# A two-layer block on one Trainium2 core: the down projection's quantising and turning of H rebuilt

## The chip, the cores and the metric

The kernel runs on one core of one Trainium2 chip. The time is the device time of one execution in microseconds (us), and the number that counts is the median over repeated executions. A core has five engines with instruction queues of their own: PE (TensorE, matrix products), DVE (VectorE), ACT (ScalarE), POOL (GpSimd) and SP (SyncE, which here only issues DMAs). They wait for each other through semaphores, and each works through its own queue strictly in order.

## What is computed

```python
x = x + tanh(g_xattn) * matmul(fake_quant(layernorm(x)), fake_quant(ctx))
x = x + tanh(g_ffn) * ffn(layernorm(x))

def ffn(x):                                   # 1024 rows, H = 1024, I = 2752
    A, g = quant_act(x)                       # blocks of 16 to fp8 with a scale; last 128 columns twice
    gate = A @ Wg.T * g;  up = A @ Wu.T * g   # weights rounded to int4 in blocks of 16
    h = silu(gate) * up
    Am, gm = quant_act(h)                     # gm = max|h| / (448 * 6), then as for A
    return Am @ Wd.T * gm

def fp8_block_qdq(v):                         # v: blocks of 16
    s = max(max|v| / 448, 1e-8)
    return float8_e4m3(v / s) * s
```

The "last 128 columns twice" are the outlier columns: they are quantised, the remainder is quantised again, and both are used against the same weight columns. The global scale gm needs the maximum over the whole of H, so no element of H can be quantised before the last one is made.

## The kernel before

The 1024 rows are eight tiles of 128 rows. Everything lives in SBUF except H, which goes to DRAM (h_d) as it is made and is loaded again tile by tile (h_in, 128 x 2752, two buffers). Weights and quantised activations are kept as two f16 numbers, a high part and the low remainder, and each product is three matmuls: high by high, high by low, low by high.

The gate and up stage makes H in units of 256 columns. The **down stage** that follows is the place of the change. For each row tile t it does this:

- scale_h (DVE) makes the block scales h_scale and the coefficients h_coef for the 172 blocks of a row: four short instructions and a reciprocal among them.
- H is multiplied by h_coef. POOL does that (line 607), except for the first 1024 columns of tile 0, which DVE does (line 1256).
- round_scaled (DVE) rounds to fp8 by the magic-constant method. power makes the constant from the exponent: line 1238 keeps the exponent bits in mgh, line 1239 applies the lower bound (a max), line 1240 adds the constant, line 1246 subtracts it, line 1247 multiplies by h_scale. Each is one pass over the part's columns. The parts are 1024 and 1728 columns in tile 0 and 2048 and 704 in the others. quantise_twice then does the outliers in twelve short instructions (lines 1263 to 1270).
- PE turns the tile (turn_piece, line 869): 22 transposes of 128 x 128 in f32 against ident, four to a PSUM bank tb. ACT copies each bank to the high part in amT (line 693) and DVE writes the low part (line 1173, lo_part).
- PE multiplies (down, line 977): 22 blocks of rows of Wd, three matmuls each, for two halves of 512 output columns: 132 matmuls a tile, 1056 in all. DVE adds the result to x (finish, line 1478) and SP stores it.

The order is written out by hand. PE does tile 0 in two groups, then for each tile: multiply half 0, turn the next tile, multiply half 1. DVE's loop (during) does for tile t: finish of tile t - 1, the six lo_part of tile t + 1, the quantising of tile t + 2 and the scales of tile t + 3. POOL's multiplication sits between scale_h and line 1238, signalled by hcoef_ready and h_scaled. am_ready tells PE that a part is quantised, hi_done and lo_done that a bank has been copied, turned that a bank is filled, y_done that a half is multiplied. Ahead of it all, line 1407 (DVE) takes the maximum of hm, which holds the block maxima, and POOL takes it across the partitions (line 601). The down projection's weights wd_hi and wd_lo were brought into their place earlier, by transposing DMAs out of nat (lines 424 and 433 of SP).

## Time and profile before

| | us |
|---|---|
| median of 3 executions | 937.62 |
| range | 936.37 to 938.55 |
| the profiled execution | 939.1 |
| its span, first to last instruction | 937.3 |

| engine | busy us | share of the span |
|---|---|---|
| PE, matmuls | 784.9 | 84% |
| PE, weight loads | 377.3 | 40% |
| DVE | 643.9 | 69% |
| ACT | 263.3 | 28% |
| POOL | 337.1 | 36% |

The last product of the gate and up stage ends at 645.3 us, so the down stage with its entry takes 292 us of the span. The profile page gives busy time by engine and by line, the share of each in the chain that ended last, and DMA traffic. The timeline lists instructions in order with the idle time before them and what ended it; PE's clock is shown as the share of full speed that was granted in a stretch, 0.50 or 1.00.

### The profile page before, as it was taken

To read this page: it belongs to the slowest core of one execution; us is meant where nothing else is said; L and a number is where in the kernel's file an instruction comes from. 1 tells how busy PE (TensorE), PEld (TensorE's weight loads), DVE (VectorE), ACT (ScalarE), POOL (GpSimd) and SP (SyncE) were. 2 spreads that over 40 slices of the span, in tenths; PEclk is the share of its full clock that TensorE was granted. 3 is DMA by queue.
4 is the path that set the end of the run, shared out by engine and by line. 5 is a ranking of instruction groups with operands and counts; after the bars stand their busy time and mean duration, and the time that the engine had idled before them with its cause. 6 is when DMAs were issued, how large, how long until landed. Compare 5 with 4: busy or idle time off the path is not lost.

```text
span 937.3 us, 11305 instructions
## 1 busy us (share of the span) xinstructions
PE 784.9 (84%) x3808; PEld 377.3 (40%) x3808; DVE 643.9 (69%) x1023; ACT 263.3 (28%) x368; POOL 337.1 (36%) x175
## 2 busy tenths in 40 slices
PE   0698100679999999999999999995589979999998
PEld 0243100445554444444444444442245434444443
DVE  5999789978767566666757667414988695976510
ACT  1964420232235353343425343300001111011000
POOL 1002054854227485665757576500302222112000
PEclk9999555789999999999999999998789999999999
DMA  7633300110038997979788897704011221121100
GB/s 288 209 103 146 130 0 0 45 62 22 20 112 184 214 196 158 221 175 224 169 198 195 194 209 167 176 28 182 1 60 61 106 104 47 60 105 45 45 23 22
DMA packets 144675, 110.32 MB, mean 118 GB/s; under 512 B 117632, under 2 KB 128896, under 8 KB 143616
## 3 DMA queue, kind: packets, MB, share of 16 engines
q1 hardware_dynamic: 144640, 109.88, 44.4%
q8 instruction: 18, 0.29, 0.1%
q14 instruction: 17, 0.14, 0.0%
HBM read 61.88 MB, written 19.66 MB: 87 GB/s over the span
## 4 chain that ended last, share of the span: by engine, by line
PE 69%; DVE 24%; issue 2%; ACT 2%; DMA 1%; POOL 1%; SPq 1%; DVEq 0%; ACTq 0%
PE acc L927 44%; PE acc L977 22%; PE tb L869 2%; DVE mid L1173 2%; DVE big L1240 1%; DVE wbuf L1167 1%; DVE bst L1065 1%; DVE h_in L1247 1%; DVE big L1095 1%; DVE h_in L1239 1%; DMA big<-in_x_dram 1%; DVE h_in L1238 1%; DVE h_in L1185 1%; DVE w_max L1155 1%; DVE h_in L1240 1%
## 5 line engine op out<-in xcount | busy, mean ns | idle before, releaser
L927 PE MATMUL acc<-mid 128*128 128x512 f16 (+1 forms) x2112 | 448.4, 375 | 0.0
L927 PEld LDWEIGHTS acc<-mid 128*128 128x128 f16 x2112 | 207.3, 98 | 239.3 <-issue 1.9
L977 PE MATMUL acc<-big,mid 128*128 128x512 f16 x1056 | 234.6, 385 | 5.2 <-DVE mid L1173 5.2
L544 POOL TENSOR_TENSOR wbuf<-wbuf,w_inv 128x1024 f32<-128x1024 f32 (+1 forms) x68 | 128.4, 1894 | 156.4 <-DVE w_inv L1161 156.4
L977 PEld LDWEIGHTS acc<-big,mid 128*128 128x128 f16 x1056 | 104.4, 99 | 132.6 <-issue 6.8
L583 POOL TENSOR_TENSOR h_in<-wbuf,h_in 128x1024 f16<-128x1024 f32 (+1 forms) x56 | 114.5, 2044 | 87.1 <-ACT h_in L784 86.9
L1311 DVE SCALAR_TENSOR_TENSOR h_out<-acc,gs,silu 128x256 f32<-128x256 f32 (+1 forms) x88 | 41.5, 471 | 119.3 <-ACT silu L742 98.3
L693 ACT ACTIVATE mid<-tb 128x512 f16<-128x512 f32 (+1 forms) x88 | 44.9, 571 | 256.4 <-PE tb L869 234.6
L607 POOL TENSOR_TENSOR h_in<-h_in,mid 128x2752 f32<-128x2752 f32 (+1 forms) x8 | 38.3, 4794 | 166.6 <-DVEq L1438 159.5
L687 ACT ACTIVATE wbuf<-wbuf 128x1024 f32<-128x1024 f32 (+1 forms) x68 | 69.1, 1017 | 99.6 <-POOL wbuf L544 98.8
L1155 DVE TENSOR_REDUCE tb<-wbuf 128x64 f32<-128x1024 f32 (+1 forms) x56 | 65.4, 1169 | 42.0 <-DMA wbuf<-in_L_ffn_w_gate_dram 23.5
L784 ACT ACTIVATE h_in<-wbuf 128x1024 f16<-128x1024 f32 (+1 forms) x56 | 57.1, 1019 | 114.9 <-DVE wbuf L1167 114.9
L1173 DVE TENSOR_TENSOR mid<-tb,mid 128x512 f16<-128x512 f32 (+1 forms) x88 | 51.9, 647 | 45.0 <-ACT mid L693 44.7
L1167 DVE SCALAR_TENSOR_TENSOR wbuf<-wbuf,tb 128x1024 f32<-128x1024 f32 (+1 forms) x56 | 65.1, 1163 | 0.3 <-issue 0.2
L742 ACT ACTIVATE silu<-acc,gs 128x256 f32<-128x256 f32 (+1 forms) x88 | 40.0, 456 | 88.8 <-PE acc L927 88.8
L869 PE MATMUL tb<-ident,big 128*128 128x128 f32 x64 | 10.9, 343 | 57.2 <-DVE big L1270 50.9
L869 PE MATMUL tb<-ident,h_in 128*128 128x128 f32 x176 | 24.6, 287 | 25.6 <-DVEq L1457 16.4
L1478 DVE SCALAR_TENSOR_TENSOR mid<-acc,gs,mid 128x512 f32<-128x512 f32 x16 | 11.5, 748 | 41.2 <-PE acc L977 39.0
L855 PE MATMUL acc<-mid,big 128*128 128x512 bf16 x128 | 32.2, 410 | 4.6 <-DVE big L1095 4.6
L1316 DVE TENSOR_REDUCE hm<-h_out 128x256 f32 (+2 forms) x88 | 34.0, 387 | 2.7
L869 PEld LDWEIGHTS tb<-ident,big 128*128 128x128 f32 x64 | 10.0, 182 | 58.1 <-DVE big L1270 51.5
L869 PEld LDWEIGHTS tb<-ident,h_in 128*128 128x128 f32 x176 | 20.1, 145 | 31.1 <-issue 19.9
(141 smaller groups left out, 594.6 us busy)
## 6 DMA issues: line engine op xcount, KB each, us to landing
h_in<-h_d SPq DMA_DIRECT2D x8, 1376.0 KB, 6.0
wbuf<-in_L_ffn_w_gate_dram SPq DMA_DIRECT2D x21, 512.0 KB, 4.3
wbuf<-in_L_ffn_w_up_dram SPq DMA_DIRECT2D x21, 512.0 KB, 4.1
h_d<-h_out SPq DMA_DIRECT2D x80, 128.0 KB, 3.4
wbuf<-in_L_ffn_w_down_dram SPq DMA_DIRECT2D x16, 512.0 KB, 4.3
wbuf<-in_ctx_dram SPq DMA_DIRECT2D x12, 512.0 KB, 4.4
big<-in_x_dram SPq DMA_DIRECT2D x8, 512.0 KB, 8.2
x_d<-big SPq DMA_DIRECT2D x8, 512.0 KB, 4.0
```

Source lines behind the costliest of these rows:

```text
L544: pool.tensor_tensor(w, w, spread(w_inv[0:rows, b, 0:cols // BLK]), ALU.mult).then_inc(w_scaled, 1)
L583: pool.tensor_tensor(nat[s % 4][:, H:H + cols], wbuf[:, s % 4, 0:cols], nat[s % 4][:, 0:cols], ALU.subtract)\
L687: act.activation(wbuf[0:rows, b, 0:cols], wbuf[0:rows, b, 0:cols], ACT.Copy, bias=MAGIC, scale=W_UP)\
L693: act.activation(dst, tb[bank][:, 0:n * P].rearrange("p (k r) -> p k r", k=n)[:, :, 0:width], ACT.Copy).then_inc(hi_done, 1)
L784: act.activation(nat[s % 4][:, 0:cols], wbuf[:, s % 4, 0:cols], ACT.Copy).then_inc(nat_hi, 1)
L869: last = pe.transpose(tb[bank][:, q * P:q * P + rows], src[0:rows, k * P:(k + 1) * P], ident[0:rows, 0:rows])
L927: last = pe.matmul(acc[m % 4][:, 0:cols], left[:, k, s * P:(s + 1) * P], ring[:, slot, right, k, 0:cols], start=(k == 0 and left is a_hi a ...
L977: last = pe.matmul(acc[2 * i + hf][:], amT[:, i, left, k, :], right[:, k, hf * MW:(hf + 1) * MW], start=(k == 0 and left == 0 and right is ...
L1155: dve.tensor_reduce(top, blocks(wbuf[0:rows, b, 0:cols]), AX_X, ALU.max, apply_absolute_value=True).then_inc(scale_step, 1)
L1167: dve.scalar_tensor_tensor(out=w, in0=w, scalar=MAGIC, in1=spread(block_scale(b, looped)[0:rows, 0:cols // BLK]), op0=ALU.subtract, op1=AL ...
L1173: dve.tensor_tensor(dst, tb[bank][:, 0:n * P].rearrange("p (k r) -> p k r", k=n)[:, :, 0:width], hi, ALU.subtract).then_inc(lo_done, 1)
L1311: dve.scalar_tensor_tensor(out=h_out[:, m % 2, 0:cols], in0=acc[m % 4][:, cols:2 * cols], scalar=gs[:, 2:3], in1=silu[:, m % 2, 0:cols], o ...
```

## The change

The down stage is written anew; nothing ahead of the last unit of the gate and up stage moves.

- **Maximum.** The maxima of all but the last 256 columns of the last tile are reduced to gpart while PE multiplies the last piece. Behind that piece DVE reduces h_out straight to one number and then four numbers to one.
- **Scales.** coef_unbound makes h_coef without gm (a clamp and a reciprocal); for tiles 0 and 1 it stands in the last unit, under PE's products. The bound by the global scale goes into the multiplication itself: min(h_coef, gs[6]) times H in one DVE pass over two inputs. POOL's multiplication is gone. h_scale is one instruction (scale_h), with the sign turned.
- **The lower bound.** The pass of line 1239 goes from DVE to ACT (floor_magic): Relu(V_UP * mg - MAGIC_FLOOR) with a bias tile floor_bias, and the two DVE passes that follow add MAGIC_FLOOR again. DVE waits for magic_floor between start_part and end_part.
- **Tiles 0 and 1** are quantised in six parts of 3, 4, 4, 4, 4 and 3 blocks of 128 columns (H_PARTS). PE still turns them, a part at a time, between the two output halves of the part before.
- **Tiles 2 to 7** are quantised in two halves of 11 blocks (1408 and 1344 columns). They are split into high and low part in natural order, by ACT (copy into nat_h, in the space of wbuf) and DVE (lo_half), and a transposing DMA of 22 blocks of 128 x 128 f16 (turn_half, SP) brings each half into amT. PE only multiplies, both output halves for columns half 0, then both for half 1.
- The loops of the stage are unrolled, and finish of tile t - 2 now stands inside the quantising of tile t.

```diff
+H_PARTS = (0, 3, 7, 11, 15, 19, DK)
+DG = len(H_PARTS) - 1
...
+MAGIC_FLOOR = 1.5 * V_UP * 2.0**-6
...
+        nat_h = wbuf[:, :, :].rearrange("p b h -> p (b h)")[:, 0:HPAD].bitcast(F16).rearrange("p (g v n) -> p g v n", g=2, v=2)
...
+            def turn_half(t, i, g):
+                if g == 0:
+                    sp.wait_ge(y_done, 2 * (t - 1))
+                sp.wait_ge(nat_h_lo, halves_before(t) + g + 1)
+                sp.dma_start_transpose(amT[:, i, g, :, :, :].rearrange("p v k r -> p (v k) r"),
+                                       nat_h[:, g, :, :].rearrange("p v n -> p (v n)")).then_inc(h_turned[g], 16)
...
+            def store_out(t, i):
+                sp.wait_ge(y_out, t + 1)
+                sp.dma_start(out_d[t], x1_t[:, i, :]).then_inc(out_stored[i], 16)
...
+            for t in range(2):
                 sp.wait_ge(turned, (t + 1) * DG + G_DOWN)
...
+                load_tile(t + 2, t)
+            for t in range(2, NT):
+                i = t % 2
+                store_out(t - 2, i)
+                turn_half(t, i, 0)
+                sp.wait_ge(out_stored[i], 16 * (t // 2))
+                load_x1(t, i)
+                turn_half(t, i, 1)
+                if t + 2 < NT:
+                    load_tile(t + 2, i)
...
-            h_times_coef(0, 0, C_FIRST)
-            h_times_coef(1, 1)
-            with pool.Fori(1, NT // 2) as it:
-                for i in range(2):
-                    h_times_coef(2 * it + i, i)
...
+            def floor_magic(n, ks):
+                mg = mgh[:, 0:min(ks.stop * P, I) - ks.start * P]
+                act.wait_ge(magic_made, n + 1)
+                act.activation(mg, mg, ACT.Relu, bias=floor_bias[:, 0:1], scale=V_UP).then_inc(magic_floor, 1)
+            for t in range(2):
+                for c in range(DG):
+                    ks = slice(H_PARTS[c], H_PARTS[c + 1])
+                    g = G_DOWN + t * DG + c
+                    if c == 0 and t == 0:
+                        floor_magic(0, ks)
+                    hi_part(g, g % 4, amT[:, t, ks.start // DH, 0, ks.start % DH:(ks.stop - 1) % DH + 1, :], ks.stop - ks.start, P)
+                    n = t * DG + c + 1
+                    if n < 2 * DG:
+                        floor_magic(n, slice(H_PARTS[n % DG], H_PARTS[n % DG + 1]))
+            act.wait_ge(nat_lo, UNITS_D * UNIT_PIECES)
+            for t in range(2, NT):
+                for g in range(2):
+                    floor_magic(parts_before(t) + g, slice(g * DH, (g + 1) * DH))
+                    act.wait_ge(am_ready, parts_before(t) + g + 1)
+                    if t >= 3:
+                        act.wait_ge(h_turned[g], 16 * (t - 2))
+                    act.activation(nat_h[:, g, 0, :], h_in[:, t % 2, g * DH * P:(g + 1) * DH * P], ACT.Copy).then_inc(nat_h_hi, 1)
...
+            def turn_h(t, c):
+                pe.wait_ge(am_ready, t * DG + c + 1)
+                g = G_DOWN + t * DG + c
+                turn_piece(h_in[:, t, :], P, range(H_PARTS[c], H_PARTS[c + 1]), g, g % 4)
...
+            turn_h(0, 0)
+            for t in range(2):
+                for c in range(DG):
+                    pe.wait_ge(lo_done, G_DOWN + t * DG + c + 1)
+                    for hf in range(2):
+                        last = down(t, hf, range(H_PARTS[c], H_PARTS[c + 1]))
+                        if c == DG - 1:
+                            last.then_inc(y_done, 1)
+                        if hf == 0 and t * DG + c + 1 < 2 * DG:
+                            turn_h((t * DG + c + 1) // DG, (c + 1) % DG)
+            for t in range(2, NT):
+                pe.wait_ge(y_out, t - 1)
+                for g in range(2):
+                    pe.wait_ge(h_turned[g], 16 * (t - 1))
+                    for hf in range(2):
+                        last = down(t % 2, hf, range(g * DH, (g + 1) * DH))
+                        if g == 1:
+                            last.then_inc(y_done, 1)
...
+            def coef_unbound(t, i, link):
+                mx, coef = hm[:, t, :], h_coef[:, i, :]
+                link(dve.tensor_scalar(coef, mx, H_SMALL, 1.0 / FP8_MAX, ALU.max, ALU.mult))
+                link(dve.reciprocal(coef, coef))
             for s in range(NT):
                 h_tile(UNITS_D, s)
+                if s == NT - 1:
+                    dve.wait_ge(h_done, (NU + 1) * NT)
+                    step(dve.tensor_reduce(gpart[:, 3:4], h_out[:, s % 2, :], AX_X, ALU.max, apply_absolute_value=True))
+                    dve.tensor_reduce(gmx[:, 1:2], gpart[:], AX_X, ALU.max).then_inc(part_max, 1)
                 h_top(UNITS_D, s)
-            dve.wait_ge(hmax_done, (NU + 1) * NT)
-            dve.tensor_reduce(gmx[:, 1:2], hm[:].rearrange("p t b -> p (t b)"), AX_X, ALU.max).then_inc(part_max, 1)
+                if s in (1, 2):
+                    dve.wait_ge(hmax_done, unit_tile(UNITS_D, s - 1) + 1)
+                    coef_unbound(s - 1, s - 1, step)
...
+                    dve.tensor_reduce(gpart[:, 0:1], hm[:, 0:s + 1, :].rearrange("p t b -> p (t b)"), AX_X, ALU.max)
+                    dve.tensor_reduce(gpart[:, 1:2], hm[:, s + 1, 0:before], AX_X, ALU.max)
+                    dve.tensor_reduce(gpart[:, 2:3], hm[:, s + 1, before + UW // BLK:NBH], AX_X, ALU.max)
...
+            step(dve.tensor_scalar(gs[:, 6:7], gs[:, 4:5], 1.0 / TINY, None, ALU.mult))
...
+            def keep_h_outliers(i):
+                step(dve.tensor_scalar(ro_h[:, i, :], h_in[:, i, I - SELECT:I], gs[:, 4:5], None, ALU.mult))
...
+            def scale_h(t, i):
+                step(dve.tensor_scalar(h_scale[:, i, :], hm[:, t, :], gs[:, 7:8], -TINY, ALU.mult, ALU.min))
...
+            def start_part(t, i, ks):
+                cs = slice(ks.start * P, min(ks.stop * P, I))
+                vb, mg = blocks(h_in[:, i, cs]), mgh[:, 0:cs.stop - cs.start]
+                v = h_in[:, i, cs]
+                step(dve.scalar_tensor_tensor(out=vb, in0=spread(h_coef[:, i, cs.start // BLK:cs.stop // BLK]), scalar=gs[:, 6:7], in1=vb,
+                                              op0=ALU.min, op1=ALU.mult))
+                dve.tensor_scalar(mg.bitcast(I32), v.bitcast(I32), 0x7F800000, 0x00400000, ALU.bitwise_and, ALU.bitwise_or).then_inc(magic_made, 1)
+            def end_part(n, i, ks):
+                cs = slice(ks.start * P, min(ks.stop * P, I))
+                v, mg = h_in[:, i, cs], mgh[:, 0:cs.stop - cs.start]
+                dve.wait_ge(magic_floor, n + 1)
+                step(dve.scalar_tensor_tensor(out=v, in0=mg, scalar=MAGIC_FLOOR, in1=v, op0=ALU.add, op1=ALU.add))
+                step(dve.scalar_tensor_tensor(out=v, in0=mg, scalar=MAGIC_FLOOR, in1=v, op0=ALU.add, op1=ALU.subtract))
+                last = dve.tensor_tensor(blocks(v), blocks(v), spread(h_scale[:, i, cs.start // BLK:cs.stop // BLK]), ALU.mult)
+                if ks.stop == DK:
+                    step(last)
+                    last = quantise_twice(h_in[:, i, I - SELECT:I].unsqueeze(1), ro_h[:, i:i + 1, :], mgh[:, 0:SELECT], step)
+                last.then_inc(am_ready, 1)
...
+            def lo_group(t, c):
+                ks = slice(H_PARTS[c], H_PARTS[c + 1])
+                at = slice(ks.start % DH, (ks.stop - 1) % DH + 1)
+                g = G_DOWN + t * DG + c
+                lo_part(g, g % 4, amT[:, t, ks.start // DH, 0, at, :], amT[:, t, ks.start // DH, 1, at, :], ks.stop - ks.start, P)
...
+            def lo_half(t, i, g):
+                dve.wait_ge(nat_h_hi, halves_before(t) + g + 1)
+                dve.tensor_tensor(nat_h[:, g, 1, :], h_in[:, i, g * DH * P:(g + 1) * DH * P], nat_h[:, g, 0, :], ALU.subtract)\
+                    .then_inc(nat_h_lo, 1)
...
+            for t in range(2):
+                reorder_max(t, t)
+                if t == 1:
+                    keep_h_outliers(1)
+                    scale_h(1, 1)
+                for c in range(DG):
+                    ks = slice(H_PARTS[c], H_PARTS[c + 1])
+                    if t == 0 and ks.stop == DK:
+                        keep_h_outliers(0)
+                    start_part(t, t, ks)
+                    if t == 0 and c == 0:
...
+                        dve.tensor_scalar(gs[:, 5:6], gs[:, 3:4], th[:, 1:2], W_DOWN, ALU.mult, ALU.mult)
+                        step(dve.tensor_scalar(gs[:, 7:8], gs[:, 4:5], -1.0 / FP8_MAX, None, ALU.mult))
+                        dve.wait_ge(hmax_done, (NU + 1) * NT)
+                        scale_h(0, 0)
+                    elif c > 0:
+                        lo_group(t, c - 1)
+                    else:
+                        lo_group(t - 1, DG - 1)
+                    end_part(t * DG + c, t, ks)
+            for t in range(2, NT):
+                i = t % 2
+                reorder_max(t, i)
+                coef_unbound(t, i, step)
+                keep_h_outliers(i)
+                scale_h(t, i)
+                start_part(t, i, slice(0, DH))
+                if t == 2:
+                    lo_group(1, DG - 1)
+                else:
+                    lo_half(t - 1, 1 - i, 1)
+                finish(t - 2, i)
+                end_part(parts_before(t), i, slice(0, DH))
+                start_part(t, i, slice(DH, DK))
+                lo_half(t, i, 0)
+                end_part(parts_before(t) + 1, i, slice(DH, DK))
+            lo_half(NT - 1, 1, 1)
+            finish(NT - 2, 0)
+            finish(NT - 1, 1)```

At the entry of the down stage PE's queue changes like this (h_in holds tile 0, tb the banks, mid the turned tile, big the weights). Before:

```order
L869 MATMUL tb<-ident,h_in 128x128 [waits am_ready,piece_turned2,lo_done,piece_turned1,piece_turned0]
L869 MATMUL tb<-ident,h_in 128x128 x3
L869 MATMUL tb<-ident,h_in 128x128 [waits lo_done]
L869 MATMUL tb<-ident,h_in 128x128 x3
L977 MATMUL acc<-big,mid 128x512 [waits lo_done]
L977 MATMUL acc<-big,mid 128x512 x47
L869 MATMUL tb<-ident,h_in 128x128 [waits lo_done,am_ready]
```

After:

```order
L898 MATMUL tb<-ident,h_in 128x128 [waits am_ready,piece_turned2,lo_done,piece_turned1,piece_turned0]
L898 MATMUL tb<-ident,h_in 128x128 x2
L1007 MATMUL acc<-big,mid 128x512 [waits lo_done]
L1007 MATMUL acc<-big,mid 128x512 x8
L898 MATMUL tb<-ident,h_in 128x128 [waits lo_done,am_ready]
L898 MATMUL tb<-ident,h_in 128x128 x3
L1007 MATMUL acc<-big,mid 128x512 x9
L1007 MATMUL acc<-big,mid 128x512 [waits lo_done]
L1007 MATMUL acc<-big,mid 128x512 x11
```

The first product needs three transposed blocks instead of eight, and the next part's transposes stand after half of a part's products.

On DVE, the rows of one steady tile (a tile 4 or later) before, from the end of one tile's outliers to the start of the next tile's rounding:

```order
L1270 TENSOR_TENSOR h_in<-h_in,mgo_a 128x128 [waits qh_step]
L1478 SCALAR_TENSOR_TENSOR mid<-acc,gs,mid 128x512 [waits y_done,x1_loaded1,am_ready]
L1478 SCALAR_TENSOR_TENSOR mid<-acc,gs,mid 128x512 [waits y_done]
L1173 TENSOR_TENSOR mid<-tb,mid 128x512 [waits hi_done] x5
L1173 TENSOR_TENSOR mid<-tb,mid 128x256 [waits hi_done]
```

After, one half of a tile (wbuf holds nat_h):

```order
L1479 SCALAR_TENSOR_TENSOR h_in<-mid,gs,h_in 128x1408 [waits dve_step]
L1481 TENSOR_SCALAR mid<-h_in 128x1408 [waits dve_step]
L1507 TENSOR_TENSOR wbuf<-h_in,wbuf 128x1408 [waits nat_h_hi]
L1516 SCALAR_TENSOR_TENSOR mid<-acc,gs,mid 128x512 [waits y_done,x1_loaded0]
L1516 SCALAR_TENSOR_TENSOR mid<-acc,gs,mid 128x512 [waits y_done]
L1488 SCALAR_TENSOR_TENSOR h_in<-mid,h_in 128x1408 [waits magic_floor]
L1489 SCALAR_TENSOR_TENSOR h_in<-mid,h_in 128x1408 [waits dve_step]
L1490 TENSOR_TENSOR h_in<-h_in,mid 128x1408 [waits dve_step]
```

The six copies out of PSUM are replaced by two of 1408 columns from SBUF (one in each half), and the wait for y_done now stands between the two sections of a part.

On PE, the queue of the last two tiles before, with the turning between the halves:

```order
L977 MATMUL acc<-big,mid 128x512 [waits lo_done,y_out]
L977 MATMUL acc<-big,mid 128x512 x65
L869 MATMUL tb<-ident,h_in 128x128 [waits lo_done,am_ready]
L869 MATMUL tb<-ident,h_in 128x128 x3
L869 MATMUL tb<-ident,h_in 128x128 [waits lo_done]
```

After:

```order
L1007 MATMUL acc<-big,mid 128x512 [waits h_turned0,y_out]
L1007 MATMUL acc<-big,mid 128x512 x65
L1007 MATMUL acc<-big,mid 128x512 [waits h_turned1]
L1007 MATMUL acc<-big,mid 128x512 x65
```

No transpose is left on PE from tile 2 on; the two waits are for DMAs.

## Rows read from the trace of the kernel before

**Rows 1.** The page: shares of the chain that ended last, by engine and line.
```profile
PE 69%; DVE 24%; issue 2%; ACT 2%; DMA 1%; POOL 1%; SPq 1%; DVEq 0%; ACTq 0%
```

**Rows 2.** Timeline of PE: start, us taken, line, operation, count, idle before.
```profile
661.66 1.94 PE L869 MATMUL tb<-ident,h_in 128*128 128x128 f32 x8 [16.40 <-DVEq L1457]
665.45 11.84 PE L977 MATMUL acc<-big,mid 128*128 128x512 f16 x48 [1.85 <-DVE mid L1173]
...
684.14 20.50 PE L977 MATMUL acc<-big,mid 128*128 128x512 f16 x84 [1.64 <-DVE mid L1173]
...
796.31 28.65 PE L977 MATMUL acc<-big,mid 128*128 128x512 f16 x132
...
827.69 28.65 PE L977 MATMUL acc<-big,mid 128*128 128x512 f16 x132
```

**Rows 3.** The chain that ended last, entry and end: start, us, what.
```profile
646.85 1.60 DVE gmx L1407
...
657.32 4.05 DVE h_in L1247
...
677.00 0.30 DVE mgo_a L1263
...
680.12 0.30 DVE h_in L1270
...
933.38 0.75 DVE mid L1478
```

**Rows 4.** Groups by form in the down stage, DVE: busy us, mean ns, idle.
```profile
L1246 DVE TENSOR_TENSOR h_in<-h_in,mid 128x1024 f32<-128x1024 f32 x1 | 1.2, 1226 | 0.0
L1247 DVE TENSOR_TENSOR h_in<-h_in,mid 128x704 f32<-128x704 f32 x7 | 6.2, 893 | 0.2
L1263 DVE TENSOR_TENSOR mgo_a<-mgo_a,h_in 128x128 f32<-128x128 f32 x8 | 2.3, 292 | 0.3
L1239 DVE TENSOR_SCALAR mid<-mid 128x2048 f32<-128x2048 f32 x7 | 8.6, 1227 | 0.2
L1238 DVE TENSOR_SCALAR mid<-h_in 128x704 int32<-128x704 int32 x7 | 3.7, 527 | 1.1 <-DVE h_in L1247 0.6
L1173 DVE TENSOR_TENSOR mid<-tb,mid 128x512 f16<-128x512 f32 x40 | 24.7, 683 | 41.9 <-ACT mid L693 41.7
L1234 DVE RECIPROCAL mid<-mid 128x172 f32<-128x172 f32 x8 | 9.8, 1228 | 0.3
L1238 DVE TENSOR_SCALAR mid<-h_in 128x1728 int32<-128x1728 int32 x1 | 4.6, 4580 | 0.0
```

**Rows 5.** Groups by form over the whole span, ACT.
```profile
L693 ACT ACTIVATE mid<-tb 128x512 f16<-128x512 f32 x76 | 41.1, 601 | 250.0 <-PE tb L869 234.6 <-PE tb L909 15.3
L784 ACT ACTIVATE h_in<-wbuf 128x1024 f16<-128x1024 f32 x48 | 50.7, 1057 | 102.4 <-DVE wbuf L1167 102.4
L784 ACT ACTIVATE h_in<-wbuf 128x704 f16<-128x704 f32 x8 | 6.3, 790 | 12.5 <-DVE wbuf L1167 12.5
L658 ACT ACTIVATE big<-big,row_term 128x1024 f32<-128x1024 f32 x8 | 8.8, 1139 | 1.1 <-DVE row_term L1114 1.0
```

**Rows 6.** Timeline of POOL: start, us taken, line, operation, idle before.
```profile
656.11 4.16 POOL L607 TENSOR_TENSOR h_in<-h_in,mid 128x1728 f32<-128x1728 f32 x1 [7.16 <-issue]
```

**Rows 7.** Two-us stretches: PE, PEld, DVE, ACT, POOL busy; clock; DMA share; GB/s.
```profile
686.00:688.00 2.00, 2.00 (x7) 0.65 (x5) 1.97 (x2) 0.00 (x0) 0.00 (x0) 0.50 0.82 341
688.00:690.00 2.00, 2.00 (x9) 0.84 (x8) 1.97 (x2) 0.00 (x0) 0.00 (x0) 0.85 0.00 0
```

**Rows 8.** Line 424's transposing DMAs (16 blocks each): issue ns, then time to landing.
```profile
L424 SPq DMA_TRANSPOSE mid<-h_in x32: 1322/2406/3801, 280.5 to 589.4; - x32
...
DMA to landing us min/median/max: 4.2/4.7/6.5
```

**Rows 9.** DMA issues by line: KB each, median us to landing (8 or 6 blocks a transpose).
```profile
h_in<-h_d SPq DMA_DIRECT2D x8, 1376.0 KB, 6.0
...
big<-h_in SPq DMA_TRANSPOSE x48, 3.7
```

193 lines of the change are left out of this document (43 added, 150 removed).

## The prediction

> **What bounds the kernel now.** I first read the chain that ended last [rows 1]: 69% PE, 24% DVE. Then PE's timeline from the last gate and up product, which ends at 645.3 us [rows 2]. Two things are to be seen there. In the middle of the stage a tile takes 31.4 us (796.31 to 827.69), 28.5 us of it 132 matmuls and 2.9 us the 22 transposes that no matmul overlaps; DVE is not late. At the entry PE waits: it idles 16.4 us before the first transposes at 661.7, starts the first 48 products at 665.45, is out of work from 677.3, and has the other 84 products of tile 0 only at 684.14. So the stage is bound by DVE until about 684 and mainly by PE afterwards. The last product ends at 933.35; then come one finish of 0.75 us [rows 3] and the store, up to 937.3.
>
> **Prices.** A DVE pass over two inputs took 292, 893 and 1226 ns for 128, 704 and 1024 columns, so 0.16 us + 1.04 ns a column; a pass over one input took 527 and 1227 ns for 704 and 2048, so 0.16 us + 0.52 ns a column [rows 4]. That gives, for 320, 384, 512, 1344 and 1408 columns, 0.49, 0.56, 0.69, 1.56 and 1.63 us (two inputs) and 0.33, 0.37, 0.43, 0.86 and 0.90 us (one). 0.03 us goes between dependent instructions. ACT took 0.60 us for a copy of 512 columns out of PSUM, and 790 and 1057 ns for 704 and 1024 from SBUF [rows 5], so 0.83 ns a column, and about 1.38 us for 1408.
>
> **The entry.** The maximum (1.60 us [rows 3]) shrinks to one over four numbers, 0.2 us, behind a reduction of 256 columns that also stood there before in another form; the rest lies in the last unit, under PE's products. gm arrives 1.4 us earlier, at 647.5. Three one-number instructions, 0.57 us, and the branch, 0.16 us, lead to 648.25. The scales with their reciprocal of 1.23 us [rows 4] are gone from here. Part 0 is 384 columns: multiply 0.56, exponent 0.37, so 649.2; ACT's floor; then three passes of 0.56. No row has this Relu. The nearest is an activation with a bias tile, 1139 ns for 1024 columns [rows 5], which at 0.83 ns a column leaves 0.60 us for 384; the low bound is the copy's 0.53, the high one 0.7. Beside it DVE has 0.6 us of small work anyway. Part 0 is ready at 651.65, where before the first part was at 661.4. That is 9.7 us, and 2.8 of them are line 1247, which took 4.05 us where a pass of this size takes 1.23 [rows 3, 4]: it stood while POOL multiplied, and so did line 1238 (4.58 us for 1728 columns, which should be 1.06 [rows 4]). POOL has nothing to do here now.
>
> The Trainium skill, page SBUF — State Buffer, section "Who interferes with whom", calls this an exclusive lock on the port pair that VectorE and GpSimd share; the trace agrees: line 1247's slow pass ends at 661.37, 1.1 us after POOL's pass, which ends at 660.27 [rows 6]. Another of its rules speaks against the change: page ScalarE: Activation LUTs, "Rules for kernel authors", wants relu, max and min on VectorE. By the prices the pass is indeed dearer on ACT (0.60 against 0.37 us, 1.45 against 0.90), but on DVE it would stand in the chain and on ACT most of it stands beside other work: by the rule part 0 would be ready 0.35 us later, not earlier.
>
> **Tiles 0 and 1.** PE turns three blocks in 0.85 us at half clock (eight took 1.94 [rows 2]), ACT copies, DVE subtracts: the first product starts at 653.8, 11.6 us earlier. Then a part of four blocks costs PE 24 x 0.216 + 0.45 for its transposes = 5.65 us. DVE needs 0.69 + 0.43 (start), 0.68 (lo_group), 3 x 0.69 (end) and gaps, 4.0 us, and the loop am_ready, transposes, copy, subtraction, end_part is 4.1 us. So PE sets the pace. What is late next are the outliers: twelve instructions from 677.00 to 680.42, 3.4 us [rows 3]. With the 320-column part's 1.56 us they come 5.0 us after lo_group of part 4, which itself is ready 1.2 us before PE takes it, so PE stands 3.8 - 2.6 = 1.2 us in tile 0. PE's clock is at half for the first 3.7 us or so of work, as before (0.50 until 688, 0.85 in the two us after, for a start at 684.14 [rows 2, 7]); that costs about 1.9 us. Sum from 653.8: part 0 with its transposes 4.4 + 2.2 (half clock), parts 1 to 3 3 x 5.65, part 4 6.75, part 5 4.2, part 6 4.35, parts 7 to 9 3 x 5.65. Part 10 starts at 709.6, call it 709.5.
>
> **Handover to the DMA.** From here DVE is the chain, since it is through with nothing of tile 2. Its time to the last lo_half of half 0, from 1.2 us before part 10: end of part 11 1.56, outliers 3.4, tile 2's branch, coefficients (0.3 + 1.23), outliers kept and scale 2.4, start of 1408 columns 2.56, last lo_group 0.55, finish 1.5, end 4.98, start of half 1 2.46, lo_half 1.66; sum 21.1, so 729.4. PE is through with tile 1 at about 722.7. Then the turning DMA. No row has 22 blocks; 16 blocks landed in 4.2 to 6.5 us, median 4.7 [rows 8], 8 or 6 blocks in 3.7 [rows 9]. I take 5.5 us, from the fastest 16 plus 6 blocks at about 0.2, since the queue is nearly empty; the bounds are 4.2 and 6.5 x 22/16 = 8.9. Tile 2 starts at 734.9. PE has idled 12 us, falls to half clock and loses another 1.9 us. Its half 1 is needed 16.1 us later, at 751.0. DVE has by then 4.8 (end) + 3.4 + 2.4 + 2.56 + 1.66 = 14.8 us, plus 5.5 for the DMA: 749.7, just in time. Both halves shift with the DMA's time, so it is paid once, at the start; only a second DMA that is over 1.3 us slower than the first shows again.
>
> **Tiles 2 to 7.** PE: 132 x 0.216 = 28.5 us, with no transposes. DVE per tile: 2.4 + 2.56 + 1.66 + 1.5 + 4.98 + 2.46 + 1.66 + 4.79 + 3.4 = 25.4 us. The new wait is finish of tile t - 2 inside tile t: behind it stand end, start, lo_half and the DMA of half 0, 10.6 + 5.5 = 16 us, for which PE's tile t - 1 gives 28.5. The SP queue holds store, turn, load of x, turn, load of H in that order; the load of H (6.0 us [rows 9]) has about 20 us until it is used. ACT's floor for a half, 1.45 us, is covered by lo_half or finish. So PE never waits, and 734.9 + 1.9 + 6 x 28.5 = 907.8. With 0.75 and the 3.2 of the store the span is 911.7, the execution 1.8 more, 913.5; the profiled execution lay 1.5 above the median, so 912. PE's switches between transposes and products in small groups are in no row; I add 1: **913 us**.
>
> **Rivals.**
>
> 1. *Handovers cost more.* Twelve parts each with 0.3 to 0.8 us more between PE, ACT and DVE, a clock that falls at the two outlier stalls (1.9 us each), a DMA of 8.9 us (3.4 at the start of tile 2). For it: the chain of tiles 0 and 1 has slack of only 1.5 us per part. Against: that slack has to go first. Time 917 to 925, centre 919.
>
> 2. *DVE becomes the bound.* The f32 minus f16 pass and the min-multiply are in no row. If they ran at twice the price, a tile would cost 25.4 + 2 x 1.6 + 2 x 1.6 = 31.8 us, 3.3 above PE's 28.5. Six tiles and the chain to tile 2 give about 913 + 20 + 4 = 937, within 0.2% of now. At a quarter more, 27.0 us, PE is still the bound and it is 914 or 915. Against it: line 1173 makes the same subtraction out of PSUM at 683 ns for 512 columns [rows 4], the normal price.
>
> 3. *Slower: the turning DMA.* It is hidden as long as it lands in 28.5 - 10.6 = 17.9 us; beyond that every us is paid in each of five tiles. The start of tile 2 pays (D - 5.5) once. The change is slower than before by over 0.2% when 939.5 - 913 = 26.5 us are lost, so when (D - 5.5) + 5 x (D - 17.9) reaches 26.5, at D = 20.3 us. The slowest row for 16 blocks is 6.5 [rows 8], so 20.3 needs 2.3 times its time per block. At 25 us it would be 968. The Trainium skill, page VectorE: DVE Perf Modes, section "The three transpose paths", has one 128 x 128 block at 1309 ns by DMA against 390 ns on TensorE and sends such turning to TensorE; as an estimate, 22 blocks one after another would be 28.8 us a half, 57.6 a tile, and about 1100 us in all. The trace does not agree for many blocks at once: 16 landed in 4.7 us [rows 8], 0.29 us each.
>
> 4. *The floor on ACT relieves nothing*, because DVE waits for it. If every floor were exposed, a tile would cost DVE 25.4 + 2 x 1.45 = 28.3 us, still under PE's 28.5, and a part of tiles 0 and 1 4.65 against 5.65. Only the chain to tile 2 would show it, 0.5 + 2 x 1.45 us and a part's floor: 917.
>
> **Chances.** The forecast (909 to 917) 0.62, rival 1 0.22, rival 2 at 937 0.03 and rival 4 0.04, rival 3 0.04, better than 909 0.05. The measurement tells 0.2%, 1.9 us, from no change; faster by more than that 0.93, within it 0.03, slower 0.04. The range of 8 in 10 is 907 to 922.
>
> **What would show it.** Right: the first product of the stage at 653 to 655; a single PE gap of 11 to 14 us near 722 to 735; then six tiles of 28.5 with no gap over 0.5 us; line 1247's kind of pass at one price throughout; turning DMAs landing in 5 to 6.5 us. Wrong: a gap in front of each tile (DMA or DVE late, and whether PE's releaser is the DMA tells which, with DVE's idle time), parts of tile 0 and 1 that take over 6.2 us, or a table load on ACT at the first floor.

## The result, and the profile after

The kernel after took 925.43 us (median of 4 runs, 924.53 to 925.83), the kernel before beside it 937.09 (936.37 to 938.55): 0.9872 of the time, 95% interval 0.9855 to 0.9889, so 11.7 us faster. The forecast was 913.0 with a range of 907 to 922. The direction was right, but less than half of the forecast 24.6 us arrived, and the time lies above the range. The profiled execution took 924.53 us, its span is 922.4.

PE's timeline of the kernel after, from the last gate and up products (line 956) to the end. Columns: start us, us taken, line and operation, count, idle before and what ended it.

```profile
649.68 7.29 PE L956 MATMUL acc<-mid 128*128 128x512 f16 x33
663.82 0.88 PE L898 MATMUL tb<-ident,h_in 128*128 128x128 f32 x3 [6.85 <-DVE h_in L1490]
665.87 4.02 PE L1007 MATMUL acc<-big,mid 128*128 128x512 f16 x9 [1.18 <-DVE mid L1184]
...
680.57 0.60 PE L898 MATMUL tb<-ident,h_in 128*128 128x128 f32 x4
681.01 5.34 PE L1007 MATMUL acc<-big,mid 128*128 128x512 f16 x24
686.19 0.60 PE L898 MATMUL tb<-ident,h_in 128*128 128x128 f32 x4
686.62 5.34 PE L1007 MATMUL acc<-big,mid 128*128 128x512 f16 x24
693.10 0.55 PE L898 MATMUL tb<-ident,h_in 128*128 128x128 f32 x3 [1.13 <-DVE h_in L1281]
...
725.73 2.75 PE L1007 MATMUL acc<-big,mid 128*128 128x512 f16 x12
730.57 5.75 PE L1007 MATMUL acc<-big,mid 128*128 128x512 f16 x18 [2.09 <-DVE mid L1184]
746.00 172.47 PE L1007 MATMUL acc<-big,mid 128*128 128x512 f16 x792 [9.68 <-DMA mid<-wbuf]
```

Three things are to be seen against [rows 2]. The stage has its new shape: one wait of 9.68 us in front of tile 2, and then 792 products, six tiles, in one piece without a gap. It takes 261.5 us from the last gate and up product to the last product (656.95 to 918.47), where the kernel before took 288.05 (645.3 to 933.35): 26.5 us are gained in the stage. And the stage starts late. The last gate and up product ends at 656.95 in place of 645.3. **So 11.65 us were lost before the first instruction that the change is about.** That is the figure of this one profiled execution; its size in the other runs is given below.

To find where, I went back along any one engine until the two kernels agreed. The shift is there at 132 us and at 38 us, and it arises in the first 23 us, on POOL. A PARTITION_ALL_REDUCE is POOL's maximum over the 128 partitions, and an IOTA writes a row of counting numbers. The kernel before (a timeline of all engines, rows of POOL and DVE):

```profile
1.08 0.14 POOL L517 IOTA iot<- 128x8 int32 x1 [0.65 <-POOLq L1527]
...
9.09 0.37 POOL L538 PARTITION_ALL_REDUCE nall<-nfl  x1 [5.65 <-issue]
9.49 0.17 DVE L1047 CAST flag<-nall 128x2 int32<-128x2 f32 x1 [2.82 <-POOL nall L538]
...
10.95 10.03 DVE L1065 BATCH_NORM_STATS2 bst<-big 128x6 f32<-128x512 f32 x16
```

The same instructions in the kernel after:

```profile
8.26 0.13 POOL L538 IOTA iot<- 128x8 int32 x1 [7.83 <-issue]
...
21.03 0.37 POOL L560 PARTITION_ALL_REDUCE nall<-nfl  x1 [10.37 <-issue]
21.44 0.17 DVE L1058 CAST flag<-nall 128x2 int32<-128x2 f32 x1 [10.69 <-POOL nall L560]
...
22.90 3.65 DVE L1076 BATCH_NORM_STATS2 bst<-big 128x6 f32<-128x512 f32 x6
```

POOL starts its first IOTA 7.2 us later, and its gap ahead of the first PARTITION_ALL_REDUCE is 4.7 us longer. DVE waits for that all-reduce with the flags, and its statistics of x stand behind them in program order: 12 us. Both gaps end in "issue": POOL waited for nothing that the profile shows. The diff touches one instruction there, a memset of 0.10 us.

POOL's table of waits in the kernel before holds the hint (engine, line, what it waited for: us in total, times, longest):

```profile
POOL gall L601 <- DVE gmx L1407: 47.4, 1, 47.4
POOL gall L549 <- DVE gmx L1210: 20.4, 1, 20.4
POOL h_in L607 <- issue: 7.2, 1, 7.2
POOL big L557 <- issue: 7.0, 1, 7.0
```

Lines 549 and 601 are the two other all-reduces, and 557 and 607 are the ordinary instructions that follow them. Each follows after 7 us of "issue". The second of these two gaps stood in the prediction's own rows, [rows 6], read there for its 4.16 us and not for its 7.16. In the built program POOL's stream has an extra instruction, PseudoReloadLibraryIndex, at these places: with index 1 ahead of every PARTITION_ALL_REDUCE, and with index 0 behind it, ahead of the next ordinary instruction, and ahead of the stream's first IOTA. This gives the theory that the runs test: **POOL changes its code there, and what is loaded at the end of one execution is still loaded when the next begins.** "Code" is read from this instruction's name: the profile has no row for it, and no packet of an instruction queue in these gaps of the two kernels. The kernel before ended POOL's stream with multiplies (line 607); the change removed them, so the stream now ends with a PARTITION_ALL_REDUCE (line 623), and the next execution's first IOTA needs the other code.

### The profile page after: what moved, and what is told of

The parts are those of the page before. It is cut to its first block, busy times and chain, and to the rows that moved or that the text cites. A ratio compares the mean times of both kernels' runs of the same rounds, so it can differ in the third digit from the quotient of the medians.

```text
span 922.4 us, 10758 instructions
## 1 busy us (share of the span) xinstructions
PE 767.1 (83%) x3676; PEld 362.8 (39%) x3676; DVE 649.2 (70%) x1036; ACT 287.5 (31%) x368; POOL 298.7 (32%) x168
## 4 chain that ended last, share of the span: by engine, by line
PE 28%; issue 25%; DVE 23%; POOL 15%; ACT 3%; SPq 3%; DMA 2%; POOLq 0%; DVEq 0%; ACTq 0%
PE acc L1007 23%; POOL wbuf L566 7%; POOL h_in L605 7%; DVE wbuf L1178 2%; PE acc L956 2%; PE tb L898 2%; DVE bst L1076 1%; DVE big L1251 1%; SPq L439 1%; DVE h_in L1250 1%; DVE h_in L1249 1%; DMA wbuf<-in_L_ffn_w_down_dram 1%; PE acc L884 1%; SPq L448 1%; DVE big L1106 1%
## 5 line engine op out<-in xcount | busy, mean ns | idle before, releaser
L956 PE MATMUL acc<-mid 128*128 128x512 f16 (+1 forms) x2112 | 449.1, 376 | 0.0
L956 PEld LDWEIGHTS acc<-mid 128*128 128x128 f16 x2112 | 207.5, 98 | 239.8 <-issue 2.8
L1007 PE MATMUL acc<-big,mid 128*128 128x512 f16 x1056 | 235.2, 385 | 12.9 <-DMA mid<-wbuf 9.7
L1007 PEld LDWEIGHTS acc<-big,mid 128*128 128x128 f16 x1056 | 104.2, 99 | 139.2 <-issue 16.1
L898 PE MATMUL tb<-ident,big 128*128 128x128 f32 x64 | 11.2, 349 | 56.6 <-DVE big L1281 50.6
L702 ACT ACTIVATE mid<-tb 128x512 f16<-128x512 f32 (+2 forms) x52 | 28.0, 575 | 85.6 <-PE tb L898 63.6
L844 ACT ACTIVATE wbuf<-h_in 128x1408 f16<-128x1408 f32 x12 | 16.5, 1377 | 93.5 <-DVE h_in L1281 49.6
L1184 DVE TENSOR_TENSOR mid<-tb,mid 128x512 f16<-128x512 f32 (+2 forms) x52 | 32.3, 654 | 16.7 <-ACT mid L702 16.5
L1516 DVE SCALAR_TENSOR_TENSOR mid<-acc,gs,mid 128x512 f32<-128x512 f32 x16 | 11.6, 746 | 41.4 <-PE acc L1007 41.4
L858 PE MATMUL tb<-identb,h_in 128*128 128x128 bf16 x64 | 6.6, 264 | 39.9 <-DVE h_in L1142 39.9
L823 ACT ACTIVATE mid<-mid,floor_bias 128x512 f32<-128x512 f32 (+4 forms) x24 | 25.3, 1056 | 31.0 <-DVE mid L1481 31.0
L898 PEld LDWEIGHTS tb<-ident,big 128*128 128x128 f32 x64 | 10.1, 184 | 57.4 <-DVE big L1281 51.1
## 6 DMA issues: line engine op xcount, KB each, us to landing
h_in<-h_d SPq DMA_DIRECT2D x8, 1376.0 KB, 7.0
```

Source lines behind the costliest of these rows:

```text
L898: last = pe.transpose(tb[bank][:, q * P:q * P + rows], src[0:rows, k * P:(k + 1) * P], ident[0:rows, 0:rows])
L956: last = pe.matmul(acc[m % 4][:, 0:cols], left[:, k, s * P:(s + 1) * P], ring[:, slot, right, k, 0:cols], start=(k == 0 and left is a_hi a ...
L1007: last = pe.matmul(acc[2 * i + hf][:], amT[:, i, k // DH, left, k % DH, :], right[:, k, hf * MW:(hf + 1) * MW], start=(k == 0 and left == ...
```

## Experiments on the late start

**One ordinary instruction at the end of POOL's stream.**

```diff
             pool.partition_all_reduce(gall[:, 1:2], gmx[:, 1:2], P, RMAX).then_inc(all_max, 1)
+            pool.iota(tail[:], pattern=[[1, 8]], base=0, channel_multiplier=8)
```

> The kernel after with one more POOL instruction behind its last all-reduce (an IOTA of 128x8 into a tile that nobody reads). The kernel after lost 11.6 us before the down stage: its POOL starts the first IOTA at 8.26 us where before it was 1.08, and the first PARTITION_ALL_REDUCE at 21.03 where before it was 9.09. Theory (code left behind): POOL has to load other code each time it goes from a PARTITION_ALL_REDUCE to ordinary instructions; the program of before ended POOL's stream with multiplies, that of after ends it with a PARTITION_ALL_REDUCE, so each execution of after starts with the wrong code. Then this kernel's first IOTA is back at 1.1 us, the all-reduce at 9.1, the last gate and up product ends at 645.3 and the time is 925.4 - 11.6 = 913.8 us. Rival 1 (the added memset of floor_bias, or the placing of the instructions in memory, shifts the start): nothing changes, 925.4. Rival 2 (only the second stall, a collision with the loads of x, matters): IOTA stays late, 925.4.

Measured: 912.95 us (912.31 to 913.56), 0.9750 of the kernel before in the same session, interval 0.9734 to 0.9766; 913.8 was expected. (Each run below is compared with a fresh measurement of the kernel before, 936.4 to 937.0 us, so differences of under 1 us between runs of different sessions say little.) POOL's timeline:

```profile
1.07 0.13 POOL L539 IOTA iot<- 128x8 int32 x1 [0.64 <-POOLq L1574]
...
9.12 0.37 POOL L561 PARTITION_ALL_REDUCE nall<-nfl  x1 [5.67 <-issue]
...
654.58 0.13 POOL L625 IOTA tail<- 128x8 int32 x1 [7.11 <-issue]
```

An instruction of 0.13 us, whose output nobody reads, at the end of the program makes its start 12 us earlier, and the last gate and up product ends at 645.20 us, as before the change. Its own gap of 7.11 us lies in the down stage, where POOL has nothing else to do. Both rivals wanted 925.4 and fall.

**The same from the other side: the kernel before, ended by an all-reduce.**

```diff
             with pool.Fori(1, NT // 2) as it:
                 for i in range(2):
                     h_times_coef(2 * it + i, i)
+            pool.partition_all_reduce(tail[:], gmx[:, 1:2], P, RMAX)
```

> The kernel before with one more PARTITION_ALL_REDUCE at the end of POOL's stream (of gmx into a tile that nobody reads). Code left behind: its next execution starts like after's, IOTA at 8.3 us and the first all-reduce at about 21, all the rest 11.6 us later, 937.1 + 11.6 = 948.7 us. Any cause that lies in the changed down stage or in the added memset: 937.1.

Measured: 948.64 us (947.45 to 948.66), 1.0128 of before, 1.0112 to 1.0145; forecast 948.7. Against the kernel before beside it (936.37) that is 12.3 us. POOL's waits in this kernel show five gaps of "issue", at the first IOTA and at each change of kind that no wait for data covers:

```profile
POOL nall L539 <- issue: 10.0, 1, 10.0
POOL iot L518 <- issue: 7.9, 1, 7.9
POOL big L558 <- issue: 7.3, 1, 7.3
POOL h_in L608 <- issue: 6.8, 1, 6.8
POOL tail L616 <- issue: 6.5, 1, 6.5
```

Nothing of the changed down stage is in this kernel, so the late start does not come from there in any other way than by what POOL's stream ends with. The last gate and up product ends at 657.04 us here. In the kernels of this study that end POOL's stream with an all-reduce and load x at once it ends at 654.9 to 657.0 us (four traces), in those that end it with ordinary work and start like the first experiment at 645.0 to 645.6 (six traces with the kernel before): the shift is 9 to 12 us. What was not tried is another program between two executions.

**The added memset.**

```diff
-            pool.memset(floor_bias[:], -MAGIC_FLOOR)
...
+            dve.memset(floor_bias[:], -MAGIC_FLOOR)
             dve.wait_ge(idx_loaded, 32)
```

> The kernel after with the memset of floor_bias made by DVE, so that POOL's instructions up to the first all-reduce are those of before one for one. Code left behind: no change, IOTA at 8.3, 925.4 us. The added instruction as the cause: IOTA at 1.1, 913.8 us.

Measured: 923.72 us (two runs, 923.22 and 924.23), IOTA at 8.31 after 7.88 us of "issue". The memset is not the cause: most of the late start stays. The time is 1.7 us under after's; 0.7 us lies between the two sessions (the kernel before took 936.37 beside this one and 937.09 beside after), and the second gap was 9.2 us in place of 10.4.

**The second gap beside the loads of x.** In the kernel after, the second change of code falls into the time in which x and ctx are loaded.

```diff
+            sp.wait_ge(flags_ready, 1)
             for t in range(NT):
                 sp.dma_start(x_all[:, t, :], x_d[t]).then_inc(x_loaded[t], 16)
```

> The kernel after with the loads of x (and so those of ctx behind them) held until the flags are made, so that no large transfer runs while POOL changes its code for the first all-reduce. In after POOL's gap ahead of that all-reduce was 10.4 us while loads of x and ctx ran, in before 5.65 us, of which the loads took only the end. If the code is fetched by the same DMA engines and had to share them, the gap shrinks to about 5.7 us, the all-reduce starts at 16.4 instead of 21.0, and the loads of x begin there; the first x tile is there some 4 us later, so the total stays within 2 us of 925.4. If the length is POOL's own, the gap stays at 10.4 us, the loads start at 21.5 and the total is 4 to 6 us longer, 930.

Measured: 924.92 us (923.45 and 926.39). POOL's timeline and DVE's:

```profile
16.90 0.37 POOL L561 PARTITION_ALL_REDUCE nall<-nfl  x1 [6.20 <-issue]
...
20.68 1.28 DVE L1077 BATCH_NORM_STATS2 bst<-big 128x6 f32<-128x512 f32 x2 [1.84 <-DMA big<-in_x_dram]
```

Without the loads the gap is 6.20 us, with them 10.37 (in the other kernels with a late start 9.2 to 10.0): the loads lengthen it by 3 to 4 us. What they share with it is not shown. As expected nothing is won by holding the loads, since x then comes late. So the loss adds up: 7.2 us for the change of code that the program's end left to do, and 3.6 to 4.7 (against the 5.65 of the kernel before) because this pushed the next change of code into the loads.

The Trainium skill, page GPSIMD Engine Reference, section "2.1 Instruction dispatch", says that the first call into a freshly loaded kernel of POOL pays a load of about 6 us with no instruction in the profile. The trace agrees for the way to an all-reduce (5.65 to 5.95 us in the kernels that start early, 6.20 with the loads held). That the way back takes 6.7 to 7.7 us, and that the start depends on how the stream ends, stands on the runs above alone, and these two are what the prediction lacked.

## Experiments on the stage's own terms

All of these start from the kernel of the first experiment, 912.95 us, in which the late start is gone. PE's last products of tile 1 and the tiles 2 to 7 in that kernel:

```profile
719.15 4.06 PE L1009 MATMUL acc<-big,mid 128*128 128x512 f16 x18 [2.09 <-DVE mid L1186]
734.58 172.65 PE L1009 MATMUL acc<-big,mid 128*128 128x512 f16 x792 [11.37 <-DMA mid<-wbuf]
```

**The lower bound back on DVE.** ScalarE's Relu is left out, and the two passes that added MAGIC_FLOOR again add 0.

```diff
-                dve.tensor_scalar(mg.bitcast(I32), v.bitcast(I32), ...).then_inc(magic_made, 1)
+                step(dve.tensor_scalar(mg.bitcast(I32), v.bitcast(I32), ...))
+                dve.tensor_scalar(mg, mg, V_UP, MAGIC_FLOOR, ALU.mult, ALU.max).then_inc(magic_floor, 1)
```

> The kernel of run e1_pool_tail (after with the IOTA at the end of POOL's stream, 912.95 us), in which the lower bound of the rounding constant is made by DVE again (multiply and maximum in one instruction behind the AND/OR) and ScalarE's Relu is gone. Theory (the floor on ScalarE is worth something only where DVE is the chain): part 0 gains 0.27 us at most, because 0.37 us more on DVE replace a Relu of 0.61 us beside which DVE had 0.6 us of small work; in tiles 0 and 1 the slack of 1.5 us a part covers it; on the chain from part 10 to the first turning DMA of tile 2, two half passes of 0.9 us, one of 0.33 and one of 0.43 are added, some of them in place of waits of 0.2: tile 2 starts 1.5 to 2.2 us later; the six tiles stay at 28.5, since DVE goes from 24.6 to 26.4 us a tile. Total 914.5 to 915.3. Rival (the floor on ScalarE relieves nothing, because DVE waits for it): 913, within 0.5 us. Rival (DVE near the bound): six tiles longer than 28.5 each, over 918.

Measured: 915.64 us (914.54 to 916.2), 0.9772 of before against 0.9750, so 2 to 2.7 us. DVE's new pass, and PE's start of tile 2:

```profile
719.12 0.90 DVE L1483 TENSOR_SCALAR mid<-mid 128x1408 f32<-128x1408 f32 x1
...
736.86 173.43 PE L1008 MATMUL acc<-big,mid 128*128 128x512 f16 x792 [10.58 <-DMA mid<-wbuf]
```

Tile 2 starts 2.3 us later than in the first experiment (734.58), 0.3 of it because the whole stage began that much later (the last gate and up product ended at 645.48 in place of 645.20), and there is no gap in the six tiles. As expected, nearly all of what ScalarE's floor is worth lies on the chain of DVE to tile 2. Not as expected, part 0 loses by the edit: PE's wait for it is 7.05 us in place of 6.85. The total lies 0.3 us above the expected range; the six tiles took 173.43 us here and 172.65 there.

**The maximum in one piece behind the last unit**, as in [rows 3].

```diff
+            dve.wait_ge(hmax_done, (NU + 1) * NT)
+            dve.tensor_reduce(gmx[:, 1:2], hm[:].rearrange("p t b -> p (t b)"), AX_X, ALU.max).then_inc(part_max, 1)
             dve.wait_ge(all_max, 2)
```

> The kernel of e1_pool_tail with the maximum over H made in one piece behind the last unit, as before the change (1376 numbers a row, 1.60 us), in place of the four parts. The prediction's term: gm 1.4 us later and everything behind it, 912.95 + 1.4 = 914.4. Rival: something else ends last in the entry (the loads of H, the coefficients), so that the maximum's 1.4 us were hidden: 913.

Measured: 914.38 us (913.85 to 915.87), 1.4 us more, and PE's wait for part 0 grew from 6.85 to 8.28 us, by the same 1.4. The term of the sum is right.

**Every turning DMA twice.**

```diff
                 sp.dma_start_transpose(...).then_inc(first_turn, 16)
+                sp.wait_ge(first_turn, 16 * (halves_before(t) + g + 1))
+                sp.dma_start_transpose(...).then_inc(h_turned[g], 16)
```

> The kernel of e1_pool_tail with every turning DMA of tiles 2 to 7 made twice, the second after the first has landed and to the same place, so that each half takes 10.4 us in place of 5.2. Theory (paid once, at the start of tile 2, hidden under 28.5 us of products afterwards): the start of tile 2 moves by 5.2 us, nothing else, 918.2. Rival (the queue of SP, where the stores and the loads of x and of H stand behind the turns, or the second half is late): 1 to 5 us more in each of five tiles, 923 to 943.

Measured: 918.93 us (917.72 and 920.13), 6.0 more with two runs. SP's first two turns and PE's start of tile 2:

```profile
728.21 3.31 SPq L507 DMA_TRANSPOSE mid<-wbuf  x1
733.43 3.35 SPq L510 DMA_TRANSPOSE mid<-wbuf  x1
...
738.72 172.97 PE L1013 MATMUL acc<-big,mid 128*128 128x512 f16 x792 [14.90 <-DMA mid<-wbuf]
```

The second turn begins 5.2 us after the first, and the products start 5.3 us after that, where in the first experiment they start 5.3 us after the only turn (issued at 729.29). So the doubling costs 5.2 us here; tile 2 starts only 4.1 us later than there because the first turn was issued 1.1 us earlier in this execution. The 792 products behind it have no gap. Up to 10.4 us a half the cost of a turn is paid once, as the prediction's third rival supposed for any duration below 17.9 us.

**POOL busy beside parts 1 and 2.** Six multiplies on the silu tile behind the IOTA.

> The kernel of e1_pool_tail with six multiplies of 128x704 f32 numbers on POOL behind its last IOTA (on the silu tile, which nobody reads any more), so that POOL is busy from 654.7 to about 667 beside parts 1 to 3 of tile 0; nothing waits for them. The prediction put 2.8 us of the old entry down to POOL's multiply beside DVE's one-input passes (4.05 us in place of 1.23). Theory: DVE's one-input passes (AND/OR, 0.43 us for 512 columns) and perhaps others take 2 to 3 times their time while POOL runs, the two-input passes do not; parts 1 to 3 have 1.5 us of slack each, so at most 1 us shows in the total, 913 to 914. Rival (DVE and POOL share nothing that matters, and line 1247's 4.05 us had another cause): all of DVE's passes at their usual price, 913. Rival (all passes slow down): parts 1 to 3 take 2 to 4 us longer each, 917 or more.

The tile's rows hold 256 columns, not 704, so POOL was busy for 4.87 us only. Measured: 913.95 us (913.75 and 914.15), 0.9757 of before, which noise does not tell from the first experiment's 0.9750. DVE and POOL:

```profile
655.11 4.87 POOL L628 TENSOR_TENSOR silu<-silu 128x256 f32<-128x256 f32 x6
655.36 0.98 DVE L1496 TENSOR_TENSOR h_in<-h_in,mid 128x512 f32<-128x512 f32 x1
656.27 1.10 DVE L1485 SCALAR_TENSOR_TENSOR h_in<-mid,gs,h_in 128x512 f32<-128x512 f32 x1
657.40 0.72 DVE L1487 TENSOR_SCALAR mid<-h_in 128x512 int32<-128x512 int32 x1
658.93 0.69 DVE L1190 TENSOR_TENSOR mid<-tb,mid 128x512 f16<-128x512 f32 x1 [0.82 <-ACT mid L708]
659.54 0.97 DVE L1494 SCALAR_TENSOR_TENSOR h_in<-mid,h_in 128x512 f32<-128x512 f32 x1
```

Undisturbed, these take 0.69, 0.75, 0.43, 0.69 and 0.69 us. Each pass out of SBUF loses about 0.3 us, with two inputs or with one; the pass with an input from PSUM loses nothing. That POOL and DVE are in each other's way is shown; that it would be the one-input passes alone is not so. The 1.2 us lost did not reach PE: from the last gate and up product to tile 2 it took 88.8 us, in the first experiment 89.4. How the 2.8 us of line 1247 [rows 3] came about, beside one long pass of POOL, was not tried.

## Experiments toward a faster kernel

**Statistics before the flags.** The late start showed that DVE's statistics of x stand behind an all-reduce that they do not need.

```diff
-            dve.wait_ge(flag_step, 5)
-            dve.tensor_copy(flag[:], nall[:]).then_inc(flags_ready, 1)
...
             aggregate(slice(0, NT))
+            dve.wait_ge(flag_step, 5)
+            dve.tensor_copy(flag[:], nall[:]).then_inc(flags_ready, 1)
```

> The kernel of e1_pool_tail with DVE's cast of the flags, which waits for POOL's first all-reduce, moved behind the statistics of x, which need no flags. In e1_pool_tail the statistics start at 10.98 us and take 9.58, without a gap. In e4_hold_x the first x tile was there 3.2 us after its load was issued and the last statistics ended 13.1 us after it; from the issue at 4.65 that is 7.9 and 17.8 us. Theory: the statistics start at about 8.3 and end at 17.8 to 18.0 in place of 20.56, all behind moves by 2.6, and the time is 910.3 us. Rival: the loads of ctx, or ScalarE behind them, end last in this stretch, and nothing or half is gained, 911.5 to 913.

Measured: 912.31 us (911.99 to 912.7), 0.9741 of before. The statistics start at 8.59 but run until 18.95, not 17.9:

```profile
8.59 8.91 DVE L1076 BATCH_NORM_STATS2 bst<-big 128x6 f32<-128x512 f32 x14 [0.58 <-DMA big<-in_x_dram]
17.66 1.29 DVE L1076 BATCH_NORM_STATS2 bst<-big 128x6 f32<-128x512 f32 x2 [0.17 <-DMA big<-in_x_dram]
```

The end was 1.6 us earlier than in the first experiment and not 2.6. There the same 16 instructions took 9.58 us without a gap; here they take 10.4, and DVE waits twice for x, as the two brackets show. In the two kernels below that keep this edit these waits come to 1.7 and 0.9 us and the statistics end at 20.0 and 19.2: the arrival of x sets part of their end now. Of the 1.6 us the profiled span shows 1.3 (909.8 against 911.1). The medians differ by 0.6, and the intervals overlap, so the gain in the time is not clear of the noise. It is half of the expected gain at most, as the rival has it, by the loads of x and not those of ctx.

**Finish of tile 0 behind the subtraction**, in tile 2 alone; SP also issues the turn before the store of tile 0.

```diff
-                finish(t - 2, i)
+                if t > 2:
+                    finish(t - 2, i)
                 end_part(parts_before(t), i, slice(0, DH))
                 start_part(t, i, slice(DH, DK))
                 lo_half(t, i, 0)
+                if t == 2:
+                    finish(0, 0)
```

> e9_stats_first with one more edit: for tile 2 alone, DVE's finish of tile 0 (1.40 us), which stands on its way to tile 2's first turning DMA, is moved behind the subtraction of half 0, beside that DMA, and SP issues the turn before the store of tile 0. Theory: tile 2 starts 1.4 us earlier than in e9, the time is 1.4 us less than e9's. Rival: the finish now stands ahead of half 1's work and its DMA is late by as much, or PE waits for the finish: no gain.

Measured: 912.85 us (912.12 to 913.41): nothing is gained. DVE after the edit:

```profile
717.35 0.55 DVE L1189 TENSOR_TENSOR mid<-tb,mid 128x384 f16<-128x384 f32 x1
719.02 1.63 DVE L1493 SCALAR_TENSOR_TENSOR h_in<-mid,h_in 128x1408 f32<-128x1408 f32 x1 [1.13 <-ACT mid L828]
```

The finish had stood in the time of ScalarE's floor (1.47 us). Without it DVE waits 1.13 us for the floor. The expectation had two rivals and neither was this one. It is the prediction's fourth rival in small: where DVE has nothing else to do, it waits for ScalarE's floor.

**The attention's maximum without POOL.**

```diff
-            pool.partition_all_reduce(gall[:, 0:1], gmx[:, 0:1], P, RMAX).then_inc(all_max, 1)
...
+            dve.tensor_copy(mgo_a[:, 0, :], gmx[:, 0:1].to_broadcast([P, P])).then_inc(max_spread, 1)
+            dve.wait_ge(max_turned, 1)
+            dve.tensor_reduce(gall[:, 0:1], tb[3][:, 0:P], AX_X, ALU.max).then_inc(all_max, 1)
...
+            pe.wait_ge(max_spread, 1)
+            pe.transpose(tb[3][:, 0:P], mgo_a[:, 0, :], ident[:]).then_inc(max_turned, 1)
```

> The kernel of e9_stats_first with POOL's second PARTITION_ALL_REDUCE (the maximum over the attention's output, L572) replaced by three instructions: DVE copies its one maximum a partition over 128 columns, TensorE transposes them, DVE takes the maximum of each row. POOL then keeps the code of ordinary instructions from its start until its last all-reduce. In e1_pool_tail that all-reduce started at 121.87 and POOL's next multiply at 129.37, 7.12 us behind it, while the coefficients it needs were there at 126.97. Theory (the change of code costs about 7 us here, of which 2.4 lie on the path): the multiply starts right behind the coefficients, 2 us earlier against the all-reduce's place (0.4 us are given back to the three instructions), and the time is 2 us less than e9's, 910.3. Rival (the seven us are hidden, because DVE or the loads end last): 912.3, no change.

Measured: 910.73 us (910.26 to 911.32), 0.9718 of before, interval 0.9702 to 0.9735; the kernel keeps the edit of the statistics. All engines around it:

```profile
119.66 0.69 DVE L1225 TENSOR_REDUCE gmx<-h_in 128x1 f32<-128x512 f32 x1
120.38 0.23 DVE L1227 COPY mgo_a<-gmx 128x128 f32<-128x128 f32 x1
...
120.66 0.47 PE L963 MATMUL tb<-ident,mgo_a 128*128 128x128 f32 x1 [8.90 <-DVE mgo_a L1227]
121.17 0.29 DVE L1229 TENSOR_REDUCE gall<-tb 128x1 f32<-128x128 f32 x1 [0.57 <-PE tb L963]
...
126.32 5.71 POOL L580 TENSOR_TENSOR big<-big,h_in 128x1024 f32<-128x1024 f32 x3 [26.28 <-DVEq L1310]
```

POOL's multiply now waits for the coefficients and for nothing else; the gap of 7 us is gone, and the multiply starts 1.3 us earlier than in the kernel with the statistics first (127.61). The time is 1.6 us under that kernel's by the medians of two sessions, 1.3 by the spans (908.5 against 909.8), where 2 were expected: what the edit gains is about a quarter of the gap. This is the fastest kernel of the study.

**The kernel after, once more, on the same chip.**

> The kernel after, unchanged, beside e11 on the same chip, so that the two can be compared. If the first IOTA at 8.3 us is part of every execution of it and not of one chip or one session: IOTA at 8.3, the first all-reduce at 20 to 21, 925.4 us. If it depends on what ran before it: between 913 and 926.

Measured: 925.12 us (924.24 to 927.71), 0.9879 of before, 0.9858 to 0.9900; IOTA at 8.35, the all-reduce at 20.54. The late start is in both measurements of this kernel, and the kernel with the transposed maximum is 14.4 us faster beside it.

## Why the prediction failed where it did

**The step that failed** stands in the paragraph on the entry. It counts from the last gate and up product at 645.3 without saying why that should stay, and it closes with "POOL has nothing to do here now". Taking POOL's multiplies out was priced by what they cost where they stood; what the end of POOL's stream does to the next start was put at nothing. They also did something by standing last: with them the next execution's first IOTA starts at 1.08 us, without them at 8.26. In the trace this is 11.65 us at the last gate and up product, and it is shown from both sides: the first experiment brings that product back from 656.95 to 645.20, the second moves it from 645.3 to 657.04. That POOL's code is what is carried over fits the built program, the gaps and the page, and remains an inference. With the late start undone the kernel takes 912.95 us against the forecast 913.0. That the two agree to 0.05 us is luck: the added 1 us for PE's switches was not needed and the span came 0.6 us below the sum (911.1 against 911.7), while the profiled execution lay 0.3 us above the median and not 1.5. No rival had it: the rivals all lay in the down stage, because the diff did. The first one's upper end, 925, meets the measured time by accident; its mechanism is answered below.

**The stage's terms**, counted from the last gate and up product (subtract 11.65 from after's times), held:

- The maximum is ready and reduced at 647.57 (forecast 647.5); one piece costs 1.4 us, as measured.
- Part 0 is ready at 651.91 (651.65), the first product starts at 654.22 (653.8). The floor for 384 columns took 0.61 us (0.60), and DVE waited 0.23 us for it. The floor on DVE made part 0 0.2 us later, where the prediction had estimated 0.35.
- A part of four blocks takes PE 5.62 us (5.65). Both outlier stalls are 1.13 and 1.14 us (1.2), and PE's clock stayed at 1.00 over the second (724 to 728 us). One stall stands in no sum: PE waits 2.09 us for the last low part of tile 1, which DVE makes behind its start on tile 2. After it the clock was 0.50 in the kernel after (732 to 734 us), and 18 products took 5.75 us; in the first experiment it was 1.00, and they took 4.06. DVE set the start of tile 2 either way, so nothing of this reached the end, and rival 1's extra microseconds a part did not come.
- SP issues the first turn at 729.07 (729.4):

```profile
740.72 3.32 SPq L505 DMA_TRANSPOSE mid<-wbuf  x1
```

- A turn lands after 5.2 us, the median of 12 (5.5); the slowest took 6.9. Tile 2 starts at 734.35 (734.9). PE idled 9.68 us in place of 12, because of the unforeseen stall and the slow products ahead of it.
- The six tiles take 172.47 us (172.9). DVE needs 24.6 us a tile (25.4): the subtraction into f16 took 1.62 us for 1408 columns (1.66), the multiply with a minimum 1.69 (1.63), 3% over the price taken, where rival 2 wanted 25 to 100%.
- From the last product to the end of the span 3.9 us (3.9).

The stage was forecast at 262.5 us and took 261.5.

Of the rivals, the third needed a DMA of over 17.9 us, and doubling it to 10.4 cost its 5.2 us once. Its break-even of 20.3 us counts one turn a tile; if the two turns of a tile follow each other in the queue, as in its own estimate of 57.6 us a tile, they would show from 14.25 us each, half of PE's 28.5. No run reached either. The Trainium skill, page VectorE: DVE Perf Modes, section "The three transpose paths", has its 1309 ns for one block; the prediction's estimate of 28.8 us a half, which multiplies it by 22, does not hold for 22 blocks in one DMA: the trace has 5.2. The second is refuted by the two prices above. The fourth, a floor that relieves nothing, is refuted too: moving the floor back to DVE cost 2 us on the chain to tile 2. Its condition showed where it was made true, when DVE's other work (the finish) was taken away and DVE waited. What the forecast put down to POOL beside line 1247 is shown in part: no pass of this kind is slowed in the kernel after, but the case itself was not repeated.

## What to carry to other kernels

A change can move time outside the stage that its diff touches: in repeated executions, which are what is timed here, an engine's last instruction in one is the neighbour of its first in the next. So before removing the last work of an engine, look at what it leaves behind, and at every "issue" gap of 7 us in the old profile, for here these gaps told where such a state changes. And when a large forecast comes in short, first compare when the changed stage starts in the two traces, before looking for the loss inside it.

## What the runs showed of the hardware that I had not expected

- POOL took 5.65 to 6.5 us from ordinary instructions to a PARTITION_ALL_REDUCE and 6.7 to 7.7 us back, without an instruction in the profile. Which of the two its stream ended with decided whether the next execution's first IOTA started at 1.1 or at 8.3 us.
- Beside loads of x and ctx the first of these took 9.2 to 10.4 us.
- Where POOL waits for data longer than the change takes, the change is hidden, ahead of an all-reduce and behind one. In the kernel after the last all-reduce started 0.14 us behind its input, which was there at 658.70:

```profile
658.84 0.38 POOL L623 PARTITION_ALL_REDUCE gall<-gmx  x1 [47.24 <-DVE gmx L1424]
```

  Behind the first all-reduce POOL waits some 68 us for DVE, and the way back shows nowhere. Behind the second the data come within 5 us, and the gap of 7 us shows.
- A maximum over partitions by a copy, a transpose and a reduction took 1.08 us from the copy's start to its end (120.38 to 121.46), the all-reduce with its handovers 0.55 us. It is the dearer one on its own and was the cheaper one here, where POOL must go back to ordinary work within 5 us.
- A turning DMA of 22 blocks landed in 5.2 us, one of 16 in 4.7 [rows 8]: 0.24 and 0.29 us a block.
